# Moving the sums of squares behind the output projection, and their readers behind the softmax sum, in a one-core attention and feed-forward kernel

## The reference

```python
# attention: 16 queries of a block see the first token and three to five neighbouring blocks (causal mask)
attn = stable_softmax(sim)                       # subtract the row maximum, exp, divide by the row sum
attn = einsum('gh,bhnij->bgnij', w_th, attn)     # heads are mixed
out  = einsum('bhnij,bhnjd->bhnid', attn, vw)
x    = layernorm(x + out @ w_out + b_out)
# feed-forward: ternary weights, each input row divided by its root mean square
def _ternary_linear(x, w):
    rms = sqrt(sum(x * x, axis=-1)) / sqrt(d)
    return (x / (rms + 1e-8)) @ w_q.T
h = gelu(_ternary_linear(x, w_up))               # 512 hidden features
x = layernorm(x + _ternary_linear(h, w_down))
```

## Time and profile before

| | before |
|---|---|
| median of 3 runs | 261.97 us (261.74 to 264.02) |
| the profiled execution | 262.22 us, of which the span of the trace is 260.3 us |
| PE busy | 227.4 us (87% of the span) |
| DVE busy | 186.1 us (71%) |
| ACT busy | 160.8 us (62%) |
| POOL busy | 91.2 us (35%) |
| mean granted TensorE clock | 0.984 |

### The profile page before, as it was taken

How to read it: one execution, slowest core, us unless ns; L and a number is a source line. 1 busy time by engine, 2 the same in 40 slices (tenths; PEclk the granted TensorE clock), 3 DMA queues, 4 the chain that set the end, 5 groups by cost and what they waited for, 6 DMA issues and landing times.

```text
span 260.3 us, 9917 instructions
## 1 busy us (share of the span) xinstructions
PE 227.4 (87%) x4291; PEld 203.7 (78%) x4291; DVE 186.1 (71%) x488; ACT 160.8 (62%) x308; POOL 91.2 (35%) x110
## 2 busy tenths in 40 slices
PE   0889986999899999999999899989999978899940
PEld 1888875898799889888888788978888767799930
DVE  0484578888866885588757795688667888885960
ACT  1475452777456655975597559755976345885840
POOL 7031522252142234353525262526352523012250
PEclk9999999999999999999999999999999999999985
DMA  6742670020002001100200110010101001000011
GB/s 227 226 119 73 200 195 4 4 63 3 3 8 57 7 18 34 35 10 16 63 3 4 43 44 23 0 43 26 41 3 43 3 3 43 1 5 21 3 43 40
DMA packets 18623, 11.69 MB, mean 45 GB/s; under 512 B 2004, under 2 KB 17940, under 8 KB 18452
## 3 DMA queue, kind: packets, MB, share of 16 engines
q1 hardware_dynamic: 17872, 9.94, 13.1%
q10 hardware_dynamic: 708, 1.12, 1.3%
HBM read 8.91 MB, written 2.10 MB: 42 GB/s over the span
## 4 chain that ended last, share of the span: by engine, by line
PE 38%; DVE 29%; ACT 22%; issue 5%; DMA 2%; POOL 1%; POOLq 0%; DVEq 0%; ACTq 0%
DVE CTl L832 8%; PE bank L1044 6%; PE bank L1046 5%; PE bank L1045 5%; DVE AT L837 4%; DVE E L846 4%; ACT Yb L551 4%; ACT E L683 3%; ACT CTh L551 3%; DVE mx L844 3%; PE bank L1189 3%; PE bank L1163 3%; ACT L634 2%; DMA xq<-in_L_attn_x 2%; DVE sm L852 2%
## 5 line engine op out<-in xcount | busy, mean ns | idle before, releaser
L832 DVE TENSOR_TENSOR CTl<-bank,CTh 128x512 fp32r<-128x512 f32 x64 | 41.1, 683 | 23.1 <-ACT CTh L551 22.8
L494 POOL TENSOR_TENSOR E<-E,rc 128x400 f32<-128x400 f32 x32 | 27.6, 864 | 81.7 <-DVE rc L854 81.7
L551 ACT ACTIVATE Yb<-bank 128x512 f32<-128x512 f32 x64 | 38.3, 599 | 21.6 <-PE bank L1046 21.0
L683 ACT ACTIVATE E<-E 128x400 f32<-128x400 f32 x32 | 17.3, 540 | 50.9 <-DVE E L846 50.9
L1044 PE MATMUL bank<-xTh,Gh 128*128 128x256 f32 x128 | 39.8, 311 | 5.6 <-ACT Yb L551 4.3
L1044 PE MATMUL bank<-CTh,Mh 128*128 128x256 f32 x128 | 36.8, 287 | 2.0 <-DVE CTl L832 1.9
L1045 PE MATMUL bank<-CTl,Mh 128*128 128x256 f32 x128 | 35.7, 279 | 0.5 <-issue 0.5
L1045 PE MATMUL bank<-xTl,Gh 128*128 128x256 f32 x128 | 35.8, 280 | 0.0
L1046 PE MATMUL bank<-xTh,Gl 128*128 128x256 f32 x128 | 35.8, 279 | 0.0
L551 ACT ACTIVATE CTh<-bank 128x512 fp32r<-128x512 f32 x64 | 34.7, 601 | 1.7 <-PE bank L1189 1.7
L1046 PE MATMUL bank<-CTh,Ml 128*128 128x256 f32 x128 | 35.7, 279 | 0.0
(11 more groups left out here) (139 smaller groups left out, 474.1 us busy)
## 6 DMA issues: line engine op xcount, KB each, us to landing
raw<-in_L_attn_x SPq DMA_DIRECT2D x37, 64.0 KB
w_sb<-in_L_attn_w_qkv ACTq DMA_DIRECT2D x2, 512.0 KB, 5.7
pt_rows<-PT SPq DMA_DIRECT2D x1, 1024.0 KB, 5.6
R<-pt_rows SPq DMA_DIRECT2D x1, 1024.0 KB, 5.1
xr<-in_L_attn_x SPq DMA_DIRECT2D x6, 128.0 KB
out<-y SPq DMA_DIRECT2D x6, 128.0 KB, 2.3
raw<-in_L_attn_x SPq DMA_DIRECT2D x12, 56.0 KB
xq<-in_L_attn_x SPq DMA_DIRECT2D x2, 256.0 KB, 5.5
```

The source lines that it names most:

```text
L494: tt(e, e, rc[s % 2][:, :].unsqueeze(2).broadcast_to([P, TILES, WIN]), ALU.mult).then_inc(s_norm, 1)
L551: copy = lambda o, i, **k: nc.scalar.activation(o, i, ACT.Copy, **k)
L683: nc.scalar.activation(e, e, ACT.Exp).then_inc(s_exp, 1)
L832: v.tensor_tensor(ct_view(CTl[s // 4 % 2], s % 4, q), c_view(s, q), ct_view(f32(CTh[s // 4 % 2][:, :, :]), s % 4, q), ALU.subtract).then_i ...
```

## The change

`square_sum(n)` moves on PE from between the first query part and `o_part` to behind `o_part`. `hidden_sum(n)` moves on DVE from ahead of `total(s)` to behind it, so that it stands directly ahead of `second_sum(n)`. `hidden_root(n)` moves on POOL from ahead of `normalise(s)` to behind it. No instruction is added or removed, none changes its size.

```diff
@@ POOL
                     if k == 4 and n < 4:
                         hidden_low(n, 0)
                         hidden_low(n, 1)
+                normalise(s)
+                for n, k in ffn(s):
                     if k == 5:
                         hidden_root(n)
-                normalise(s)
-                for n, k in ffn(s):
                     if k == 0:
                         variance_roots(n)
@@ DVE
                 shift(s)
                 for n, k in ffn(s):
-                    if k == 5:
-                        hidden_sum(n)
                     if k == 2:
                         layernorm(n)
                 total(s)
                 for n, k in ffn(s):
                     if k == 5:
+                        hidden_sum(n)
                         second_sum(n)
@@ PE
                 if s == 0 or s >= O_LAG:
                     queries(s, 0)
-                for n, k in ffn(s):
-                    if k == 5:
-                        square_sum(n)
                 if s == O_LAG:
                     pe.wait_ge(s_eva, read_no("A", "m", 3))
                     pe.wait_ge(s_evd, read_no("D", "m", 3))
                 for part in o_parts(s):
                     o_part(*part)
+                for n, k in ffn(s):
+                    if k == 5:
+                        square_sum(n)
```

## The result

The change makes the kernel slower, as forecast, but by more than three times as much: 284.6 us median (284.1 to 285.0, 6 runs) against 262.24 us of the kernel before on the same chip. The ratio is 1.0835 with a 95% interval of 1.0797 to 1.0873; the forecast of 269.0 with its range up to 271.0 is missed. The profiled execution took 285.0 us, its span is 283.1 us (before 262.22 and 260.3), its mean granted TensorE clock 0.942 (before 0.984).

What follows compares the result with a forecast made beforehand. No single engine bounds the kernel; in the four changed steps whatever delays hden on DVE delays x1Tl and PE. Four steps by 1.71 us is 6.84 us on 262.22, said as 269.0 us, range 266.6 to 271.0.

Steps and rivals of the forecast that it cites:

- PE, the square sums: PE, steps 16, 20, 24, 28: sums end later, but the softmax covers that before hss needs them; price nothing.
- DVE, place left: DVE ahead of the row sum: removing hss gains nothing, since the sum waits for ACT; at most 0.15 us a step.
- POOL, normalisation: POOL: the normalisation waits for rc with hroot already done, so it starts no sooner; gain nothing.
- DVE and POOL, place taken: Steps 16, 20, 24, 28: hroot waits behind the normalisation, so hden on DVE starts 1.71 us later in each.
- The length of hden: DVE, the four changed steps: hden starts later but keeps its 0.13 us.
- POOL, behind: POOL behind the root: xw starts 0.69 us later, but relatively sooner for the loads it releases; price nothing.
- The clock follows: Rival: PE's idle time of about 1.9 us before the up projection lowers its clock, adding 2.7 us: 271.7; chance 3%.
- Given back in part: Rival: later slack in the four slots takes up half of each stall, giving 265.6 us; chance 7%.
- The range: Whole kernel: forecast time between 266.6 and 271.0 us, with 84% for each step paying its wait nearly in full.
- upper bound of 271.2: Four steps at 2.24 us each, with a slower root, longer normalisation and slower hand-over: 9.0 us more.

Runs made afterwards that it cites:

- run 5: Kernel before with only the PE part of the change (square sums behind the output projection): 262.3 us, ratio 1.0006.
- run 11: Kernel before with only the DVE part of the change (hss behind the softmax sum), and hden of chunks 0 to 3 through PSUM: 265.95 us, ratio 1.0103.
- run 10: run 8 with 9 more matmuls on PE ahead of the transposition of x1n in steps 20 and 24: 270.0 us, ratio 1.0259.
- run 7: Kernel before with only the DVE part of the change (hss behind the softmax sum, root still ahead of the normalisation on POOL): 271.6 us, ratio 1.0341.
- run 9: Changed kernel with POOL's subtraction xw cut into two instructions of half the size: 278.0 us, one execution.
- run 2: Changed kernel with hden of chunks 0 to 3 written to PSUM and read there by the reciprocal: 274.0 us, ratio 1.0434.
- run 8: Changed kernel with hden through PSUM and extra matmuls in PE's waits (17 before up projection in steps 17, 21, 25; 25 in step 29): 271.0 us.
- run 3: Changed kernel with extra matmuls in PE's waits (36 before the up projection in steps 17, 21, 25; 44 in step 29): 278.1 us, ratio 1.0597.

## Why the prediction missed

By its own steps:

- **PE, the square sums: nothing.** Right (run 5: 262.3 against 262.1). hss never waits for PE in the four steps.
- **DVE, place left, and POOL, normalisation: nothing.** Nothing in the runs speaks against it; neither was tried by itself. With hss gone from its place, the row sum's wait for ACT became 0.61 us instead of 0.54, so it starts no sooner, as the prediction has it.
- **DVE and POOL, place taken: hden 1.71 us later.** Right to the hundredth: hden starts at 125.13, less the 0.98 that the execution was already behind, that is 124.15. Run 11 shows the same kind of term at another size, and run 10 that the four of them make the time (7.2 us against 6.8) once the two other effects are taken away.
- **The length of hden.** This is the step that failed. The prediction moved the start of hden and kept its 0.13 us. In the kernel before, hden starts at 122.44, 0.16 us ahead of the normalisation at 122.60; POOL has nothing running. After the change it starts 0.06 us behind xw. The prediction had both times, since it put the start of xw 0.69 us after that of hroot, and priced this under **POOL, behind** at nothing, for what waits for xw; it did not ask what runs beside xw. 8.7 us.
- **What it drew on.** The prediction used the Trainium skill's "SBUF — State Buffer", section Who interferes with whom, to judge whether DVE could slow down the moved root. The same section of the Trainium skill says that the blocking goes both ways: a VectorE tensor_scalar between SBUF operands can enter a mode that uses the ports which it shares with GpSimd, and whichever of the two engines comes first keeps them for its whole instruction. Runs 7 and 9 agree for POOL coming first, with hden at 0.82 and 1.22 us; the other order stands in none of the rows here. The Trainium skill's "VectorE: DVE Perf Modes", section Why PSUM operands drop a tier, adds that an operand in PSUM rules that mode out. Run 2 agrees, with 0.16 us beside xw; the mode itself shows in no row.
- **The clock follows: 3%, at most 2.7 us.** The mechanism was named, its price and chance were wrong. It was set aside because one idle time of 1.86 us left the clock at 1.00. In run 2 an idle time of 1.91 us has the clock at 0.50 behind it, in the profile of run 8 one of 1.16 us does, and of two of 1.77 us in run 7 one does and the other does not. The length of the idle time alone thus does not decide it, and one row was too little to rule it out. The price was put on 8 matmuls; in the changed kernel PE stays at 0.50 for some 5 us in step 17, over the up projection, the first queries and the output projection. This is the second step that failed: 6.4 us in the profile, 6.5 by run 3.
- **Given back in part.** Not in the changed kernel: in the sum above each later start of hden reaches the end in full. In run 11 the slots in the profile show nothing given back either (0.98 or 0.99 us more in each); its median, 3.1 us above before, leaves room for a little.
- **The range.** Its upper end, 271.0, lies a little under the prediction's own upper bound of 271.2. That changes nothing here: neither holds the hold-up of hden or the slower clock in four steps.

The two misses are linked. Held for 2.17 us more, hden lengthens PE's wait from 1.9 to 4.05 us. But the clock would have cost without it too: in run 2, with the forecast wait alone, it is most of what lies between 269 and 274.0, since runs 8 and 10, which keep PE at work in such waits, bring the time to 271.0 and 270.0.

What stays open: which idle times of PE bring the clock down, and why the executions of run 8 differ in it. No row here tells the two waits of 1.9 us, in run 2 and in the kernel before, apart, or the two of 1.77 us in run 7.

## What to carry to other kernels

When an instruction is moved, ask not only what it waits for and who waits for it, but also which instructions of the other engines will be running at its new place. Here a DVE tensor_scalar of two numbers in each partition, from SBUF to SBUF, that landed 0.06 us behind the start of a long POOL operation lasted as long as that operation. Where such an instruction can't be moved, another form can help: with its destination in PSUM it took 0.16 us (run 2), and with the POOL operation cut in two 1.22 us (run 9). And a new idle time on TensorE is priced with the slower clock behind it as a bound of the range, not as a rival of 3%.

## What was not expected of the hardware

- A DVE tensor_scalar of 128 x 2 fp32, SBUF to SBUF, took 2.30 us beside a POOL tensor_tensor of 2.34 us that had started 0.06 us earlier; the profile counts the time in which it was held as busy time, so it shows as a long instruction and not as a wait. The reciprocal behind it, of the same size and also in SBUF, is not held: in run 7 it took 0.17 us from 125.38, with xw on POOL from 125.27.
- With two POOL instructions back to back (run 7), the waiting DVE instruction got its turn when the first ended.
- The granted clock fell to 0.50 behind idle times of PE of 4.05 us (changed kernel), 1.91 (run 2), 1.77 (run 7, step 25), 1.16 and 1.00 (profile of run 8), and not behind 1.86 in the kernel before, 1.77 in step 21 of run 7 or 1.60 in run 11. The same idle time, at the same place of the loop in the same execution, can do either.
